# Graph attention, two layers, on one core: ScalarE's instructions within a step in another order

## The reference

```python
for i in range(2):
    h = layer_norm(x, ln1_g[i], ln1_b[i])
    xl = (h @ Wl[i] + bl[i]).reshape(n, 2, 128); xr = (h @ Wr[i] + br[i]).reshape(n, 2, 128)
    e = leaky_relu(xl[src] + xr[dst], 0.2)
    score = einsum("ehd,hd->eh", e, att[i])
    ex = exp(score - segment_max(score, dst)[dst])
    alpha = ex / (segment_sum(ex, dst)[dst] + 1e-16)
    g = segment_sum(xl[src] * alpha[..., None], dst).reshape(n, 256) + gat_b[i]
    x = x + (g @ proj_W[i] + proj_b[i])
    h = layer_norm(x, ln2_g[i], ln2_b[i])
    x = x + (gelu(h @ W1[i] + b1[i]) @ W2[i] + b2[i])
```

## The kernel before

| engine | order in step i |
|---|---|
| TensorE | pieces of tiles (normalized rows L1153 and L1157, down projection L1161); scores i-1; projection i; sums i-5; pieces of tiles (staging L1143, L1115, L1120, up projection L1126, L1132); transposes of exponentials i-4 |
| ScalarE | `wgt` i-5; relus i-1; pieces of tiles (identities L1214, L1220 and L1230, root L1242, tanh L1254, bias copies and square L1262 and L1267); `hold_s` i-2; exponential i-4; `lin` i; pieces of tiles (stage L1294, squares L1302 and L1308, splits) |
| VectorE | adds i-6; pieces of tiles; minimum i-3; one-hot i+1; pieces of tiles (reciprocals, L1530, L1533, GELU product L1537) |

## Time and profile before

### The profile page before, as it was taken

The page is one execution under the profiler, slowest core; times in us unless marked ns, Lnnn a source line. Parts: engine busy times, 40 slices in busy tenths (PEclk is TensorE's granted clock), DMA queues, the critical chain, the costliest instruction groups (busy, mean ns, idle before and its releaser), DMA issues. The chain is left out here.

```text
span 2743.9 us, 66371 instructions
## 1 busy us (share of the span) xinstructions
PE 1964.3 (72%) x19001; PEld 1307.1 (48%) x19001; DVE 1302.8 (47%) x5318; ACT 1411.6 (51%) x3474; POOL 1543.5 (56%) x1664
## 2 busy tenths in 40 slices
PE   4567777777777777777744777777777777777775
PEld 2234555554554555545533445544545545555453
DVE  7324554554544544544541344444444444444445
ACT  4324555555555555555542455555555555555554
POOL 4656666565566566565315666566556565565540
PEclk9778988989999998998966898999998999889997
DMA  5544444444454454444214444444444444444430
GB/s 133 166 111 127 127 130 128 132 130 128 130 131 128 129 132 129 128 133 128 73 56 117 122 125 128 126 121 129 128 125 128 123 125 127 125 124 128 124 107 7
DMA packets 236750, 332.67 MB, mean 121 GB/s; under 512 B 51011, under 2 KB 160491, under 8 KB 236395
## 3 DMA queue, kind: packets, MB, share of 16 engines
q0 software_dynamic: 75072, 208.30, 29.4%
q1 hardware_dynamic: 161322, 120.16, 14.9%
HBM read 308.02 MB, written 20.25 MB: 120 GB/s over the span
## 5 line engine op out<-in xcount | busy, mean ns | idle before, releaser
L982 POOL DMA_INDIRECT rows<-table,src_t x1564 | 1492.5, 954 | 995.5 <-PE psum L1182 367.9
L1428 DVE SCALAR_TENSOR_TENSOR acc<-acc,keep,psum 128x129 f32 x782 | 273.2, 349 | 1164.2 <-PE psum L1182 596.9
L1207 ACT COPY wgt<-psum 128x256 f32<-128x256 f32 x392 | 146.0, 373 | 1030.2 <-PE psum L1190 649.4
L1089 PE MATMUL psum<-lz,att_w 128*32 128x256 f32 x3128 | 281.2, 434 | 513.6 <-ACT lz L1200 444.6
L1103 PE MATMUL psum<-ident,rows 128*128 128x128 f32 x3128 | 578.4, 315 | 34.9 <-DMA rows<-table,src_t 34.9
L1103 PEld LDWEIGHTS psum<-ident,rows 128*128 128x128 f32 x3128 | 412.3, 160 | 237.5 <-issue 187.8
L1200 ACT ACTIVATE lz<-psum 128x512 f32<-128x512 f32 x782 | 427.8, 603 | 41.0 <-DMA table<-row 14.4
L1182 PE MATMUL psum<-rows,wgt 128*32 128x129 f32 x6256 | 313.8, 302 | 49.3 <-issue 45.9
L1089 PEld LDWEIGHTS psum<-lz,att_w 128*32 128x32 f32 x3128 | 64.4, 113 | 590.0 <-ACT lz L1200 509.4
L1106 PE MATMUL psum<-oh,xrw 96*128 96x256 bf16 x1564 | 344.4, 306 | 0.0
L1279 ACT ACTIVATE ex<-hold_s,peak 128x256 f32<-128x256 f32 x392 | 201.5, 514 | 138.4 <-issue 87.4
(11 more groups left out here) (257 smaller groups left out, 2100.1 us busy)
## 6 DMA issues: line engine op xcount, KB each, us to landing
xrw<-xr_split SPq DMA_DIRECT2D x782, 48.0 KB
relb<-rel_d SPq DMA_DIRECT2D x194, 192.0 KB
rows<-table,src_t POOLq DMA_INDIRECT x1564
relb<-cyc_d SPq DMA_DIRECT2D x194, 64.0 KB
xr_split<-split SPq DMA_DIRECT2D x50, 192.0 KB, 1.9
table<-row SPq DMA_DIRECT2D x50, 130.0 KB, 2.1
x_mid<-x SPq DMA_DIRECT2D x25, 64.0 KB
xo<-x_mid SPq DMA_DIRECT2D x25, 64.0 KB
```

Source lines behind the costliest of these rows:

```text
L982: pool.indirect_dma_start(rows[:, ring(u), t, u % M, :, :].rearrange("p h c -> p (h c)"), None, s["tables"][layer][0:NP, :], bass.Indirect ...
L1089: m = pe.matmul(out[o:o + W, 0:UE], w["att_w"][:, h * W:h * W + W], lz[:, u % M, h * UE:h * UE + UE], start=False, stop=True, skip_group_c ...
L1428: m = v.scalar_tensor_tensor(a, a, s["keep"][:, u:u + 1], sum_bank(i - 6)[:, c:c + D + 1], ALU.mult, ALU.add)
```

## The change

ScalarE's step i is put in another order, and three of its parts work on a later step of edges. TensorE's order stays.

| ScalarE's step i | before | after |
|---|---|---|
| 1 | `wgt` i-5 | identities of tiles |
| 2 | relus i-1 | relus i |
| 3 | identities of tiles | `wgt` i-4 |
| 4 | root, tanh, bias copies and square | the same |
| 5 | `hold_s` i-2 | exponential i-3 |
| 6 | exponential i-4 | `hold_s` i-1 |
| 7 | `lin` i, rest | the same |

VectorE's `lowest` goes from i-3 to i-2. `lz` gets four buffers in place of two, so the relu's wait for the scores that last read its buffer is one step looser.

```diff
-    lz = sb("lz", [P, M, H * UE], F32)
+    lz = sb("lz", [P, 2 * M, H * UE], F32)
...
-                                      lz[:, u % M, h * UE:h * UE + UE], start=False, stop=True, skip_group_check=True)
+                                      lz[:, u % (2 * M), h * UE:h * UE + UE], start=False, stop=True, skip_group_check=True)
...
-                hold(act, score_ready, u // M)
-                act.activation(lz[:, u % M, :], ps[u % M][:, :], ACT.Relu).then_inc(lz_ready, 1)
+                hold(act, score_ready, u // M - 1)
+                act.activation(lz[:, u % (2 * M), :], ps[u % M][:, :], ACT.Relu).then_inc(lz_ready, 1)
 
             for i in range(END):
-                new = of_step(i - 1)
-                if of_step(i - 5):
-                    act.wait_ge(ex_turned, i - 4)
-                    hold(act, sums_ready, i - 6)
-                    act.copy(wgt[:, (i - 5) % 2, :, :].rearrange("p t c -> p (t c)"), ps[4][:, 0:UE]
-                             ).then_inc(wgt_ready, 1)
-                for u in new:
-                    relu(u)
...
+                for u in of_step(i):
+                    relu(u)
+                if of_step(i - 4):
+                    act.wait_ge(ex_turned, i - 3)
+                    hold(act, sums_ready, i - 5)
+                    act.copy(wgt[:, (i - 4) % 2, :, :].rearrange("p t c -> p (t c)"), ps[4][:, 0:UE]
+                             ).then_inc(wgt_ready, 1)
...
-                new = of_step(i - 2)
+                old = of_step(i - 3)
+                if old:
+                    n, c = len(old) * HW, (i - 3) % 4
+                    act.wait_ge(max_ready, min(i - 1, NO))
+                    hold(act, ex_turned, i - 4)
+                    act.activation(ex[0:n, (i - 3) % 2, :], hold_s[0:n, c, :], ACT.Exp, bias=peak[0:n, c:c + 1],
+                                   scale=-1.0).then_inc(ex_ready, 1)
+                new = of_step(i - 1)
                 if new:
                     n = len(new) * HW
-                    act.wait_ge(score_ready, i - 1)
-                    hold(act, ex_ready, i - 5)
-                    act.copy(hold_s[0:n, (i - 2) % 4, :], scores(i - 2)[0:n, 0:UE]).then_inc(held, 1)
-                old = of_step(i - 4)
-                if old:
-                    n, c = len(old) * HW, (i - 4) % 4
-                    act.wait_ge(max_ready, min(i - 2, NO))
-                    hold(act, ex_turned, i - 5)
-                    act.activation(ex[0:n, (i - 4) % 2, :], hold_s[0:n, c, :], ACT.Exp, bias=peak[0:n, c:c + 1],
-                                   scale=-1.0).then_inc(ex_ready, 1)
+                    act.wait_ge(score_ready, i)
+                    hold(act, ex_ready, i - 4)
+                    act.copy(hold_s[0:n, (i - 1) % 4, :], scores(i - 1)[0:n, 0:UE]).then_inc(held, 1)
                 new = of_step(i)
                 if new:
+                    hold(act, score_ready, i - 1)
                     for u in new:
                         act.wait_ge(rows_in[u % ROWS], (u // ROWS + 1) * (16 * K))
-                    hold(act, score_ready, i - 1)
...
-                if of_step(i - 3):
-                    lowest(i - 3)
+                if of_step(i - 2):
+                    lowest(i - 2)
```

## The result

The change made the kernel slower by a third: 3020.4 us (median of 4 runs, 3016.7 to 3023.1) against 2266.6 (2265.6 to 2268.6), ratio 1.333 (95% interval 1.331 to 1.335). The direction and the wait that takes the relus' place were as forecast; the price of the slower clock was not, and 2745 and the range up to 2890 were too low.

The account below looks back on a forecast made before the run. It took the loop of transposes, weights' copy, relus, attention matmuls and the rest of TensorE's step as the bound. Median 2266 + 414 (196 + 76 + 54 + 88) + 68 = 2748, said as 2745 us; range 2580 to 2890.

Parts of the forecast that it names:

- plain wait for `lin`: TensorE's scores wait for `lin`, queued behind weights' copy, exponential and scores' copy: +0.50 us per step, 392 steps, +196 us.
- bias copies and square: ScalarE's tile work between the weights' copy and `lin` comes onto the loop: 44 x 1.72, +76 us.
- tanh, product, down projection: Tanh, VectorE's product and TensorE's down projection stand ahead of the scores: 1.22 us over a plain step, 44 times, +54 us.
- root, less the exponential's wait: Root's two table loads before `lin` add 3.02 us; 1.01 of transposes' waiting is given back: net 2.01, 44 times, +88 us.
- point 5: TensorE's clock: one step at 1.2 GHz behind each square root, 44 x 1.54 = 68 us; bounds nothing and 120.
- point 3: ScalarE's tile work between copy and `lin` comes onto the loop in three of eight steps: +76, +54 and +88 us.
- Table loads: Around the square root on ScalarE: two loads of 1.28 us each, without the skill page's added drain of about 1.38 us.
- Stalls that soak up the waits: Rival: 1.0 us slack per step absorbs the plain wait, leaving 218 us of tile work, time 2484 us; chance 0.08.
- Loads dearer by 113 us: Rival: each of 88 table loads on the loop costs another 1.28 us, +113, time 2861 us; chance 0.03.
- The clock falls for good: Rival: most TensorE steps run at 1.2 GHz, +460 us, time 3140, or 2910 with half of that; chance 0.08.
- The faster case: Rival: relus' 1.41 us wait goes and `lin` is not late; capped by the gathers at about 2230 us; chance 0.04.
- The gathers as a common pace: Rival: GpSimd's gathers pace both kernels, so the order makes no difference, 2266 us; chance 0.02.

Follow-up runs that it names:

- e3b: Changed kernel with TensorE given useless identity matmuls in all its waits for `lin`, beside a before of 2265.7 us: 2693.4 us, 1.189.
- a2: The changed kernel as it stands, no further edit, with its trace: 3021.0 us.
- e10: Kernel before with 3 identity products added per step ahead of the wait for the relus, output wrong: 2777.6 us, 1.012 of before at 2746.8.
- e8: Changed kernel with only the waits behind bias copies and behind tanh filled with identity products, beside a before of 2746.8 us: 3135.5 us, 1.143.
- e8b: Repeat of e8 for a chip on which before takes 2266 us: 2902.1 us, 1.283.
- e1: Changed kernel with `lin` moved to the head of ScalarE's step, ahead of its relus, beside a before of 2709.5 us: 2944.7 us, 1.087.
- e1b: Repeat of e1 beside a before of 2265.7 us: 2340.7 us, 1.033.

## Why the prediction was wrong

The terms of its sum, with what the runs at 2266 measured:

| term | forecast | measured |
|---|---|---|
| plain wait for `lin`, 392 steps | 0.50 each, 196 | 0.65 each (5.15 less 4.50), 255 |
| bias copies and square, 44 | 1.72 each, 76 | 1.70 (3.76 less 2.06, e3b), 75 |
| tanh, product, down projection, 44 | 1.22 each, 54 | 1.16 (3.22 less 2.06), 51 |
| root, less the exponential's wait, 44 | 3.02 - 1.01, 88 | 3.02 - 1.08 (5.58 less 4.50), 85 |
| sum | 414 | 427 (2693.4 less 2266) |
| clock | 68 | 328 (3021.0 less 2693.4) |

**The wait for `lin` in place of that for the relus: right.** The place, the queue behind the copy of the weights and the three kinds of tile work are in the trace as foretold, and moving `lin` undoes it. The plain wait was 0.15 us short: 0.10 for the handover from ScalarE to TensorE (`lin` ends at 1391.32, the transposes start at 1391.47; I took 0.05), 0.03 for lin's transposes and masks (0.57 for 0.54) and 0.02 for `lin` itself (0.41 for 0.39). The single terms add up to 466, 39 more than the measured 427; by the starts of the copies about half of that lies in steps 16 to 183, above all since before's step behind the root takes 5.18 and not 4.50 in the first layer, and the other half in the first 16 and last 11 steps of each layer, which in both kernels differ from the plain ones. The kernel before has a little of the slow clock too (64 of the 2016 us of its two stretches, 791 of 2774 in a2), so 427 and 328 are not the sums at full clock on both sides; the run that was to give before at full clock (e10) fell beside a before of 2747.

**The clock, point 5: the step that failed.** "I take one such step behind each square root: 44 x 1.54 = 68", with "a fifth of all steps (78 x 1.54 = 120)" as the upper bound. The price of a slow step, 1.54, was near: behind the root it takes 1.70 us more than with the wait filled (9.87 less 8.17). The number of such steps was wrong, one per tile where the runs show four: of a tile's eight steps four are slow in the changed kernel, those behind the root, the bias copies and tanh and the up projection's, together 6.4 of the 6.7 us per tile between the two columns. The bound was wrong as well, since it took the 0.90 of the front profile as the most that such waits could do. That trace had on average 1 us of gaps per step; waits of 3 to 5 us in three steps of eight are another thing. The forecast had those lengths in its own point 3 and did not carry them to point 5. By the page "TensorE: Matmul & The Clock Gate" of the Trainium skill, section "A second HAM failure mode: psum-queue depth-cycling", short idle stretches between groups of matmuls made the clock of a kernel go up and down, and by it the rival of the slower clock was to be likelier than by the rows. The traces agree: the clock goes up and down within each tile, and its mean is 0.961 before and 0.854 after.

**Table loads: right by the trace.** The loads on the loop cost 1.28 us each and nothing beside it; the drain of about 1.38 us that the page "ScalarE: Activation LUTs" of the Trainium skill adds, section "What ACT_TABLE_LOAD costs", is not seen (root 1.29 us after its load's start, exponential 1.30 after the second's).

**The rivals.** Stalls that soak up the waits: no, the kernel before at 2266 takes 5.17 us per step and has no room for them. Loads dearer by 113 us: no, by the rows above. The clock falls for good (3140, or 2910 with half of it): this came nearest, between its two times, and had been given 0.08; the clock falls in four steps of eight, not for good. The faster case: its mechanism (early relus with a punctual `lin`, capped by the gathers at about 2230) was real, at 2212.5 and so 18 us under its cap, but only in another order. The gathers as a common pace: no, by the halved gathers.

## What to carry to other kernels

When an instruction is moved behind a wait on another engine's end of step, everything queued after it moves with it: the instruction that the other engine needs first must stand ahead of the wait. Here the relus' 0.9 us were won and `lin`'s 1.5 lost, and the tiles' work with its table loads, which had cost little in a wait (1.08 us at each root), came onto the loop. And price a wait on TensorE twice: once for its length, once for the steps behind it at the lower clock; filling the waits with idle products, without touching the order, told the two apart (427 and 328 us).

## What the runs showed of the hardware

Useless matmuls made a kernel faster by 328 us of 3021, where they kept the granted clock of the two stretches at 1.00 in place of 0.88 and 0.85, and the plain waits for `lin` and those behind the root stayed as long.

The kernel before has two times, 2266 and 2710 to 2750, in sets of runs that can lie minutes apart, and one chip showed both. The longer one is not in its transfers: the gathers' packets took 29.4% of 2743.9 us and 35.6% of 2266.0, both 807 us. In it ScalarE's copy of the weights starts on average 0.67 us after TensorE's last transposes do, not 0.31, and from the start of the weighted sums to that of the next burst it is 0.98 us, not 0.74. The changed kernel itself was never timed beside a before of 2700 or more; its variants were, and took 233 to 604 us longer there than beside 2266 (e8 and e8b, e1 and e1b). What brings it on stays open.
